# The second input-gate matmul of a gated-linear-attention layer, moved behind the eight transposes of x

## What is computed

```python
x = hidden @ up_w.T                      # 256 -> 512
final_gate = hidden @ gate_w.T
shift = silu(causal_conv4(x) + conv_b)
q, k = shift @ q_w.T, shift @ k_w.T      # 64 keys
v = sigmoid(x @ ig_w1.T @ ig_w2.T + ig_b2) * x      # the input gate
g_gate, tau = softplus(shift @ g_w.T + g_b), sigmoid(shift @ tau_w.T + tau_b)
kn = k / norm(k) * g_gate ** tau
o = gated_linear_attention(q / 8, kn, v, -g_gate * tau) + shift * residual_weight
o = rmsnorm(o * silu(final_gate)) * norm_weight
attn = o @ down_w.T
# feed-forward: 256 -> 1024 (gated), 1024 -> 1024 (h1), 1024 -> 1024 (h2), 1024 -> 256 (w3)
h = silu(x @ w1.T * s1) * (x @ w2.T * s2)
h = gelu(h @ h1.T * sh1); h = gelu(h @ h2.T * sh2)
ffn = h @ w3.T * s3
```

## Time and profile before

| | |
|---|---|
| median of 3 runs | 2006.12 us (2004.93 to 2006.96) |
| the profiled execution, its own time | 1999.92 us |
| its span, first to last instruction | 1998.1 us |
| TensorE busy | 1980.6 us (99%) |
| weight loads busy | 1961.1 us (98%) |
| VectorE busy | 1575.6 us (79%) |
| ScalarE busy | 1256.9 us (63%) |
| granted TensorE clock, mean | 0.998 |

### The profile page before, as it was taken

One profiled execution on the slowest core, in us unless ns is written; L12 is line 12 of the kernel. 1 busy time (PEld: TensorE's weight loads), 2 busy tenths in 40 slices (PEclk: granted clock), 3 DMA queues, 4 the chain that ended last, 5 costly groups with the idle time before them and its releaser, 6 DMA issues.

```text
span 1998.1 us, 46801 instructions
## 1 busy us (share of the span) xinstructions
PE 1980.6 (99%) x17508; PEld 1961.1 (98%) x17508; DVE 1575.6 (79%) x4242; ACT 1256.9 (63%) x2495; POOL 68.4 (3%) x104
## 2 busy tenths in 40 slices
PE   7999999999999999999999999999999999999998
PEld 7999999999999999999999999999999999999998
DVE  7787778877788877787877788777788777878777
ACT  5665656666556666566656566656566665666564
POOL 0000000000000000000000000000000000000000
PEclk9999999999999999999999999999999999999999
DMA  8000000000000000000000000000000000000000
GB/s 300 7 12 12 12 7 6 12 12 11 12 1 11 12 12 12 11 1 12 12 12 12 12 1 12 12 11 12 2 11 12 12 12 11 1 12 11 12 7 7
DMA packets 23360, 34.22 MB, mean 17 GB/s; under 512 B 2945, under 2 KB 19713, under 8 KB 23186
## 3 DMA queue, kind: packets, MB, share of 16 engines
q1 hardware_dynamic: 23186, 31.46, 4.7%
HBM read 23.07 MB, written 8.39 MB: 16 GB/s over the span
## 4 chain that ended last, share of the span: by engine, by line
PE 95%; issue 2%; DVE 1%; SPq 1%; ACT 0%; DMA 0%; POOLq 0%; POOL 0%; DVEq 0%; ACTq 0%
PE fb L363 63%; PE ab L363 25%; PE ab L567 3%; PE ab L509 1%; PE ab L497 1%; PE ab L433 1%; PE fb L648 1%; PE ab L560 0%; SPq L271 0%; PE ab L559 0%; DVE hid0l L937 0%; DMA small<-stage_w 0%; PE ab L558 0%; SPq L276 0%; PE ab L423 0%
## 5 line engine op out<-in xcount | busy, mean ns | idle before, releaser
L363 PE MATMUL fb<-hid1h,wwhole 128*128 128x256 f32 x2048 | 474.2, 279 | 0.0
L363 PE MATMUL fb<-hid1l,wwhole 128*128 128x256 f32 x2048 | 469.1, 277 | 0.0
L363 PE MATMUL fb<-hid0l,wwhole 128*128 128x256 f32 x2048 | 467.6, 277 | 0.0
L363 PE MATMUL fb<-hid0h,wwhole 128*128 128x256 f32 x2048 | 467.5, 276 | 0.0
L363 PEld LDWEIGHTS fb<-hid1h,wwhole 128*128 128x128 f32 x2048 | 384.7, 188 | 2.2
L363 PEld LDWEIGHTS fb<-hid1l,wwhole 128*128 128x128 f32 x2048 | 384.7, 188 | 0.0
L363 PEld LDWEIGHTS fb<-hid0l,wwhole 128*128 128x128 f32 x2048 | 384.7, 188 | 0.0
L363 PEld LDWEIGHTS fb<-hid0h,wwhole 128*128 128x128 f32 x2048 | 384.7, 188 | 0.0
L801 ACT ACTIVATE raw<-fb,sh_s 128x256 f32<-128x256 f32 x512 | 212.5, 466 | 129.7 <-PE fb L363 128.4
L363 PE MATMUL fb<-xnth,wwhole 128*128 128x256 f32 x1024 | 237.7, 276 | 0.0
L363 PE MATMUL fb<-xntl,wwhole 128*128 128x256 f32 x1024 | 237.5, 276 | 0.0
(11 more groups left out here) (210 smaller groups left out, 4604.6 us busy)
## 6 DMA issues: line engine op xcount, KB each, us to landing
xin<-x SPq DMA_DIRECT2D x32, 256.0 KB, 2.7
out<-xin SPq DMA_DIRECT2D x32, 256.0 KB, 2.2
stage_more<-stage_w SPq DMA_DIRECT2D x6, 512.0 KB, 7.2
sgate<-stage_w SPq DMA_DIRECT2D x4, 512.0 KB, 5.1
shift<-stage_w SPq DMA_DIRECT2D x4, 512.0 KB, 5.4
v<-stage_w SPq DMA_DIRECT2D x4, 512.0 KB, 5.8
raw<-stage_w SPq DMA_DIRECT2D x3, 512.0 KB, 6.1
mixed<-stage_w SPq DMA_DIRECT2D x3, 512.0 KB, 8.4
```

The lines of the kernel that those rows point to most:

```text
L363: mm = pe.matmul(o, a, b, start=start and i == 0, stop=stop and i == len(pairs) - 1)
```

## The change

One call is moved in TensorE's program.

```diff
                     layer1(m)
-                input_gate(1)
 
                 for c in range(NC):
                     pe.wait_ge(x_ev.sem, x_ev.at(me))
                     for d in range(DB):
                         mm = pe.transpose(ab[c][:, d * P:(d + 1) * P], xbuf[:, d, W - 1 + c * CH:W - 1 + (c + 1) * CH], ident_s[:])
                     mm.then_inc(xt_mm.sem, 1)
+                input_gate(1)
 
                 pe.wait_ge(shift_hi.sem, shift_hi.at(me))
```

## The result

The changed kernel took 1987.69 us (median of 4 runs, 1986.30 to 1989.81), the kernel before 2005.53 us (median of 4 runs, 2004.21 to 2006.96; three of them are the runs of the first table). The ratio is 0.991, with a 95% interval of 0.9898 to 0.9923: faster, by 17.8 us. The forecast was 1997.1 with a range from 1988 to 2003.

A forecast was written before the change was run, and what follows sets the result against it. TensorE's own stream, busy 99% of the span, was taken as the bound. Wait -6.7, junctions +0.6 and pace -2.9 made -9.0 us, from a median of 2006.1 to 1997.1 us, range 1988 to 2003.

The forecast's parts named there:

- The wait: Line 497's weight load waits for ScalarE's line 735; eight transposes moved ahead cover it: 6.7 us gained.
- The junctions: Transposes into line 497, then line 497 into the projection: 0.6 us lost.
- The upper bound: At the junction of transposes into line 497, a load not hidden: 0.10 us a half, 3.2 us in all.
- The slack of zero at partl: Projection's first load behind VectorE's partl write: 25th half 0.03 us late, 24th 0.05 on time; taken as nothing, bound 0.4 us.
- The rule of weight loads: Loads overlap matmuls only in other row groups: would make the wait's gain 3.6 us, the sum 2000.2; not followed.
- The pace: Projection, h1 and h2: three halves at slow spacing turn fast behind a 512-column matmul, 2.9 us gained.
- The sum: Whole kernel: -6.7 + 0.6 - 2.9 = -9.0 us, against the profiled execution of 1999.92 us, so 1990.9.
- I carry the difference over: Median before, 2006.12 us, lies 6.2 us above its profile; the same was assumed after, giving 1997.1 us.
- The w3 rival: w3 and down projection turn fast in 27 halves without the wait: 6.8 us more gained, 1990.3 us; chance 0.13.
- The range: Whole kernel: 1988 to 2003 us, held at 8 in 10, taking in unchanged pace, fast w3 and the junction's upper bound.

The follow-up runs named there:

- e2: Kernel before with its matmul order kept; ScalarE evaluates gate bank 1 earlier, ahead of its wait for the convolution: 1985.52 us, ratio 0.9923 to the kernel before.
- e4: Kernel before with the second input-gate matmul placed between the transposes of chunk 0 and chunk 1: 1988.16 us, ratio 0.9935 to the kernel before.
- e6: Changed kernel with ScalarE evaluating gate bank 1 later, behind input_gate(0) and hid0(1), so the wait returns: 2010.60 us, ratio 1.0046 to the kernel before.
- e5: Changed kernel plus an overwritten 512-column matmul between the four transposes and w3 in every half: 2000.03 us, ratio 1.0000 to the kernel before.
- e3: Changed kernel with ScalarE evaluating gate bank 1 ahead of its wait for the convolution: 1988.19 us, ratio 0.9944 to the kernel before.
- e9: Changed kernel again, without edit, on another comparison's chip: 1987.70 us, ratio 0.9923 to the kernel before.
- e8: As e2, plus an overwritten matmul of 16 rows out and 256 columns ahead of w3 in second halves: 1989.29 us, ratio 0.9947 to the kernel before.
- e10: e2 again, without further edit, on another chip: 1986.05 us, ratio 0.9915 to the kernel before.
- e11: As e10, but the second input-gate matmul stands between the two chunks' transposes in second halves only: 1981.87 us, ratio 0.9900 to the kernel before.
- e12: As e10, but the second input-gate matmul stands between the two chunks' transposes in first halves only: 1989.88 us, ratio 0.9938 to the kernel before.
- e1_before_again: Kernel before, without edit, run and traced again: 2001.62 us, ratio 1.0001 to the kernel before.
- e7_after_again: Changed kernel, without edit, run and traced again: 1990.54 us, ratio 0.9951 to the kernel before.

## Why the prediction was right in direction and wrong in size

**The wait: right, and well sized.** 6.7 us were forecast. Against e2, which differs from before only in that nothing waits, a first half before is 0.247 us longer from the first input-gate matmul to the projection's seventh and a second half 0.174, over 31 halves 6.5 us.

**The junctions: right.** 0.6 us lost was forecast, 0.6 was measured (7 and 33 ns a half). The upper bound, an exposed load in each half, didn't come. One sign was missed: the projection's first matmul comes 0.32 us behind line 497's, not 0.23 to 0.26, but its second then follows by 0.12 us, where it was 0.21 before.

**The slack of zero at partl: right.** The forecast had the 25th half's load late by 0.03 us and at no cost; it is held, by 0.07, at no cost. The time from VectorE's end to the load is 0.07 us there, not the 0.05 that I took from ScalarE. For the 24th half I had put 0.13 us where the 25th has 0.11; with 0.11 its slack is 0.03 us, still enough, and second halves aren't held. But the zero was only right for the load's own place, as the pace shows.

**The rule of weight loads.** The forecast set the Trainium skill's rule (TensorE: Matmul & The Clock Gate, What overlaps and what doesn't), that a load overlaps a matmul in flight only in other row groups, against the rows, and went by the rows. The rule would have given 3.6 us for the wait; 6.5 were measured. This case's traces disagree with it: loads of 128 rows start 0.11 us apart beside matmuls that start 0.11 us apart too.

**The pace: the right sign for the wrong reason.** I wrote that the three slow halves would go because a 512-column matmul would lead into the projection. e2 and e4 have no slow piece with transposes there; e6 has 14 with the 512-column matmul there; e5 turned a fast stretch slow with one. What goes with slow pieces is a held load. The traces with the wait of line 497 have three, nine and fourteen slow h1 pieces. The eleven without it have five together, and those five stand in the traces of the changed order on TensorE (e3, e5, e9), each in a first half, where partl holds the projection's load by 0.07 us. In the six traces in which neither of these loads is held (e2, e4, e8, e10, e11, e12) none of 192 pieces is slow, and none of the 80 second halves of the five traces of the changed order, which have the same order without the holding. So the holding that I had put at nothing goes, in 5 of the 72 halves that have it, with 0.7 to 0.9 us more in that half. These are counts of one execution each, and why a held load leaves some junctions in the slow spacing is not shown.

**The sum: the step that failed is "I carry the difference over".** The time came 9.4 us below the forecast, and 4.8 of them are this step. The median before lay 6.2 us above its own profile, and I took that as a constant that the changed kernel would have too; its median lies 1.4 us above its profile. The 6.2 us were no constant. The kernel before had medians from 2000.1 to 2005.5 us on the chips here, and e1_before_again, traced at 2003.61 us, has nine slow pieces where the first trace has three, so at least a part of them is pace. The executions near 2006 were not traced, and 1999.92 us isn't one of the runs behind the median, so how much was pace stays open. Nor is the 1.4 a constant: in e7_after_again the trace without a slow piece is 3.7 us below the median.

**What the sum left out between the profiles.** The other 4.6 us are 13.6 us between the two profiles where 9.0 were forecast. w3, which the sum put at nothing, gave 2.9. The clock's fall in the first trace, which no step of mine looked at, gave 1.7, and that is luck of the one execution. The other stages gave 1.3. Against them the wait and the junctions gave 5.7 and not 6.1, and the slow pieces 2.0 and not 2.9, since a stall in the 31st half's h2 took 0.8 back.

**The w3 rival came half.** At 0.13 I had given "w3 turns fast too" for all halves, at 6.8 us. It turned fast in first halves and stayed slow in second ones, 2.9 us. Its reason, that the stream runs alone without the wait, isn't what decides: e11 and e12 show that a half's own order does.

**The range.** Its lower end took in the fast w3, but not the fast w3 together with a smaller distance from profile to median. In one of the three comparisons the gain, 9.6 us, was near the forecast 9.0. So how far the size was off depends also on how the kernel before happened to run.

## What to carry to other kernels

When an engine is busy 99% of the span, a wait of 0.2 us that the list of waits half hides is worth looking for: compare the start-to-start distances of the same place in several halves with an undisturbed one. Before moving work behind a wait, see whether its releaser has idle time to run earlier; here that gave the same gain with one activation moved on ScalarE, and steadier runs: e2 and e10 spread over 2.4 and 1.9 us, the changed kernel over 3.5, 5.3 and 3.7. If the median of the runs lies above the profiled execution, ask what differs between executions before adding the difference to a forecast: if it is the pace of the stream, a change at a junction may take it away.

## What the runs showed of the hardware that was not expected

- A long stretch of 256-column matmuls, each with its own weight load, keeps one of two spacings at full clock: 128 of them in 14.51 or 15.08 us. Within a stretch it stays the same (0.113 or 0.118 us from start to start in the 25th and 27th half before), and it can be different in executions of one kernel (three and nine slow ones in two traces).
- The order of nine small matmuls decides over the spacing of a stretch 40 us later in the same half: with the 512-column matmul between the transposes w3 is fast in second halves and slow in first ones, with it at either end of them the other way round. Choosing by half gave 4.2 us. The mechanism stays open.
- A load of a matmul behind a 512-column matmul may come 0.07 us late without delaying its own matmul: the two are 0.32 us apart either way. Yet the five slow h1 pieces of the changed order all stand behind such a load.
